# Scatter of the routed rows: 4 groups by 32 slot pairs, two 64-token products side by side, 4 KB row pieces

## The reference

```python
# layer 0, routed feed-forward: groups of 16 tokens, 64 slots a group
grouped = x.reshape(..., 16, d)
logits = einsum('...btd,des->...btes', grouped, controller) + tie
perm = (logits == max(logits, axis=-3, keepdims=True))      # which token fills a slot
sel = einsum('...btd,...btes->...besd', grouped, perm)
inner = relu(einsum('...besd,desf->...besf', sel, f1) + bias)
inter = einsum('...besf,esfd->...besd', inner, f2)
out = einsum('...besd,...btes->...btd', inter, perm)         # the scatter
x = x + tanh(g_ffn[0]) * out
# layer 1: softmax(layernorm(x) @ ctx.T / sqrt(512) + mask * -1e9) @ ctx, added to x;
# then a layer norm and an int8/ternary feed-forward whose scale is a quantile of |h|
```

## Time and profile before

| | value |
|---|---|
| median of three runs | 1633.4 us (1632.84 to 1636.59) |
| the profiled execution: its span | 1630.0 us, core 0, mean granted TensorE clock 0.894 |
| `phase2b3`, first to last instruction | about 845.4 to 1158.4 us |
| busy share of the span | PE 81%, DVE 63%, ACT 47%, POOL 27% |
| scatter products, L1197 | 256 records (two for each of 128 f32 products), 131.5 us |
| row loads, L1131 | 128 DMAs of 256 KB, median 5.5 us from issue to landing |

### The profile page before, as it was taken

One profiled execution on the slowest core, in us unless ns is written; L12 is line 12 of the kernel. 1 busy time (PEld: TensorE's weight loads), 2 busy tenths in 40 slices (PEclk: granted clock), 3 DMA queues, 4 the chain that ended last, 5 costly groups with the idle time before them and its releaser, 6 DMA issues. The chain is left out here.

```text
span 1630.0 us, 24926 instructions
## 1 busy us (share of the span) xinstructions
PE 1327.1 (81%) x8930; PEld 934.2 (57%) x8930; DVE 1032.4 (63%) x2374; ACT 759.7 (47%) x1145; POOL 432.6 (27%) x435
## 2 busy tenths in 40 slices
PE   6999999999999738999957999996141799343996
PEld 5787888878888527666524666664041444142442
DVE  5577666766667533444334778786496399776774
ACT  3233333333333212665333555554383655386991
POOL 1233333333323310110012787866100000000011
PEclk9999999999999968999978999998555699755998
DMA  6111222111221158787589988860300177421973
GB/s 217 46 66 67 73 84 103 65 71 66 94 93 40 40 213 293 261 300 271 219 305 278 256 238 231 235 183 29 121 1 3 78 310 305 162 78 51 419 311 149
DMA packets 100406, 261.79 MB, mean 161 GB/s; under 512 B 11120, under 2 KB 22480, under 8 KB 93136
## 3 DMA queue, kind: packets, MB, share of 16 engines
q1 hardware_dynamic: 88704, 226.82, 40.1%
q0 software_dynamic: 8688, 32.51, 5.8%
q10 hardware_dynamic: 2912, 1.14, 0.3%
HBM read 155.32 MB, written 105.12 MB: 160 GB/s over the span
## 5 line engine op out<-in xcount | busy, mean ns | idle before, releaser
L1197 PE MATMUL p_s<-p_rows,p_permT 128*128 128x512 f32 x256 | 131.5, 611 | 5.9 <-DMA p_rows<-inter_d 3.9
L916 PEld LDWEIGHTS p_sel<-p_pick,p_xp 128*128 128x128 bf16 x1536 | 89.5, 100 | 55.5 <-issue 34.2
L916 PE MATMUL p_sel<-p_pick,p_xp 128*128 128x128 bf16 x1536 | 100.9, 224 | 21.9 <-DMA p_xp<-xparts 19.3
L2261 POOL DMA_DIRECT2D p_y<-residual x8 | 10.0, 1254 | 405.4 <-POOLq L113 342.9
L1928 PE MATMUL p_z<-qT,w1T 128*128 128x512 bf16 x512 | 113.3, 385 | 2.1 <-PEq L113 2.1
L1054 DVE COPY p_selT<-p_sel 128x512 f32<-128x512 f32 x64 | 44.2, 691 | 104.5 <-PE p_sel L916 104.5
L2285 PE MATMUL p_o<-w2T,p_Gq 128*128 128x512 bf16 x384 | 85.9, 384 | 8.0 <-DVE p_Gq L2342 8.0
L1987 DVE MAX8 cand<-hid 128x8 f32<-128x128 f32 x384 | 74.7, 276 | 25.1 <-ACT hid L1975 25.1
L1928 PEld LDWEIGHTS p_z<-qT,w1T 128*128 128x128 bf16 x512 | 50.6, 99 | 64.7 <-issue 5.7
L999 ACT ACTIVATE p_selT<-p_sel 128x512 f32<-128x512 f32 x64 | 38.2, 597 | 88.3 <-PE p_sel L916 88.3
L341 PE MATMUL p_M<-p_ctxTh,p_Wkh 128*128 128x256 f32 x256 | 76.0, 297 | 1.9 <-DVE p_Wkl L663 1.9
(11 more groups left out here) (335 smaller groups left out, 3935.3 us busy)
## 6 DMA issues: line engine op xcount, KB each, us to landing
inter_d<-p_stage SPq DMA_DIRECT2D x64, 512.0 KB, 4.1
p_rows<-inter_d SPq DMA_DIRECT2D x128, 256.0 KB, 5.5
activations<-hid SPq DMA_DIRECT2D x24, 1024.0 KB, 3.9
p_cin<-in_ctx_dram SPq DMA_DIRECT2D x32, 512.0 KB, 5.1
xparts<-p_parts SPq DMA_DIRECT2D x16, 768.0 KB, 3.2
hid<-activations SPq DMA_DIRECT2D x10, 1024.0 KB, 9.1
p_xp<-xparts SPq DMA_DIRECT2D x3, 3072.0 KB, 24.9
p_xin<-in_x_dram SPq DMA_DIRECT2D x16, 512.0 KB, 4.2
```

The costliest lines, as they stand in the source:

```text
L916: mm = pe.matmul(bsel[u % 2][:, k * P:(k + 1) * P], xp[:, c, tile, r, :], pick[sb % 2][:, tile, :, :].rearrange("p s g -> p (s g)"), start ...
L1197: mm = pe.matmul(bo[t][:, :], permT[b % 2][:, t, k, :], R[b % 2][:, t, k, :], start=(k == 0), stop=(k == NK - 1))
```

## The change

Each tile's 512 rows are cut another way. The tile is halved, h = 0 and 1, by its groups (4 groups, 64 tokens each), and the slots go in pairs q = 0, 1. A block of 128 rows is 4 groups x 32 slot pairs, the same q of each pair, so a product of a block writes only the 64 tokens of its own half. Two such products, of h = 0 and h = 1, write partitions 0 to 63 and 64 to 127 of one bank, one issued right behind the other; two q accumulate. That is again 8 products per batch, each of 64 weight columns. `spread` and `permT` have half as many values (256 per token and tile), with a mask of 4 columns that DVE sums from the old one once; `turn_perm` has 4 transposes for 8. A tile's rows come by one DMA of 1 MB in 256 pieces of 4 KB, contiguous in DRAM, 2 DMAs per batch for 8.

```diff
-SK = 16
-NK = SL // SK
+GH = 4
+TH = P // 2
+ND = 2
...
-        rows = inter_d.rearrange("(n g) (k s) d -> n k s g d", g=GR, s=SK)
+        rows = inter_d.rearrange("(n h g) (s q) d -> n (g s) h (q d)", h=2, g=GH, q=ND)
...
             def load_rows(b, t):
-                for k in range(NK):
-                    sp.dma_start(R[b % 2][:, t, k, :], rows[b * NT + t, k]).then_inc(s[f"r_in{b % 2}{t}"], 16)
+                sp.dma_start(R[b % 2][:, t, :, :, :].rearrange("p h q d -> p h (q d)"), rows[b * NT + t]).then_inc(s[f"r_in{b % 2}{t}"], 16)
...
-                mm = pe.matmul(bo[t][:, :], permT[b % 2][:, t, k, :], R[b % 2][:, t, k, :], start=(k == 0), stop=(k == NK - 1))
-                if k == NK - 1:
+                for h in range(2):
+                    toks = slice(h * TH, (h + 1) * TH)
+                    mm = pe.matmul(bo[t][toks, :], permT[b % 2][:, t, q, toks], R[b % 2][:, t, h, q, :], start=(q == 0), stop=(q == ND - 1))
+                if q == ND - 1:
...
-                for k in range(NT * NK):
+                for k in range(NT * ND):
                     if i < B:
-                        scatter(i, k // NK, k % NK)
+                        scatter(i, k // ND, k % ND)
                     if k == 0 and live(i - 2):
                         scores(i - 2, 1)
-                    if k == 1 and i + 1 < B:
+                    if k == 0 and i + 1 < B:
                         turn_perm(i + 1)
-                    if k == 3 and live(i - 2):
+                    if k == 2 and live(i - 2):
                         turn_e(i - 2)
-                    if k == 4 and live(i - 1):
+                    if k == 2 and live(i - 1):
                         turn_xn(i - 1)
-                    if k == 5 and live(i - 2):
-                        attend(i - 2, 0)
-                    if k == 6 and live(i - 2):
-                        attend(i - 2, 1)
-                    if k == 6 and i < B:
-                        turn_ctx(i)
-                    if k == 7 and live(i - 1):
-                        scores(i - 1, 0)
+                if live(i - 2):
+                    attend(i - 2, 0)
+                    attend(i - 2, 1)
+                if i < B:
+                    turn_ctx(i)
+                if live(i - 1):
+                    scores(i - 1, 0)
...
+            pool.wait_ge(s["mask4_done"], 1)
...
+            dve.tensor_tensor(mask4[:, :], gmask[:, 0:GH], gmask[:, GH:GR], ALU.add).then_inc(s["mask4_done"], 1)
```

More of the change, by code:

```diff
@@ L1085, in phase2b3 @@
         sbt = lambda n, s, d=F32: es.enter_context(nc.sbuf_tensor("p3_" + n, s, d))
-        R = [sbt(f"rows{i}", [P, NT, NK, D]) for i in range(2)]
+        R = [sbt(f"rows{i}", [P, NT, 2, ND, D]) for i in range(2)]
         xy = [sbt(f"xy{i}", [P, NT, D]) for i in range(XD)]
-        spread = [sbt(f"spread{i}", [P, NT, SL, GR], BF16) for i in range(2)]
-        permT = [sbt(f"permT{i}", [P, NT, NK, P]) for i in range(2)]
+        spread = [sbt(f"spread{i}", [P, NT, ND, GH, SL // ND], BF16) for i in range(2)]
+        permT = [sbt(f"permT{i}", [P, NT, ND, P]) for i in range(2)]
+        mask4 = sbt("mask4", [P, GH])
         ident, identb = sbt("ident", [P, P]), sbt("identb", [P, P], BF16)
@@ L1188, in _, with scatter @@
         def _(pe):
-            def scatter(b, t, k):
-                if t == 0 and k == 0:
+            def scatter(b, t, q):
+                if t == 0 and q == 0:
                     pe.wait_ge(s["permT_done"], b + 1)
-                if k == 0:
-                    pe.wait_ge(s[f"r_in{b % 2}{t}"], 16 * NK * (b // 2 + 1))
+                if q == 0:
+                    pe.wait_ge(s[f"r_in{b % 2}{t}"], 16 * (b // 2 + 1))
                     if b >= 1:
                         pe.wait_ge(s["added"], NT * (b - 1) + t + 1)
-                mm = pe.matmul(bo[t][:, :], permT[b % 2][:, t, k, :], R[b % 2][:, t, k, :], start=(k == 0), stop=(k == NK - 1))
-                if k == NK - 1:
+                for h in range(2):
+                    toks = slice(h * TH, (h + 1) * TH)
+                    mm = pe.matmul(bo[t][toks, :], permT[b % 2][:, t, q, toks], R[b % 2][:, t, h, q, :], start=(q == 0), stop=(q == ND - 1))
+                if q == ND - 1:
                     mm.then_inc(s["scattered"], 1)
@@ L1205, in turn_perm @@
                 for t in range(NT):
-                    for k in range(NK):
-                        mm = pe.transpose(bP[:, :].bitcast(BF16)[:, (t * NK + k) * P:(t * NK + k + 1) * P],
-                                          spread[b % 2][:, t, k * SK:(k + 1) * SK, :].rearrange("p s g -> p (s g)"), identb[:, :])
+                    for q in range(ND):
+                        mm = pe.transpose(bP[:, :].bitcast(BF16)[:, (t * ND + q) * P:(t * ND + q + 1) * P],
+                                          spread[b % 2][:, t, q, :, :].rearrange("p g s -> p (g s)"), identb[:, :])
                 mm.then_inc(s["turned"], 1)
@@ L1289, in permT_out @@
                     act.wait_ge(s["scattered"], NT * (b - 1))
-                act.activation(permT[b % 2][:, :, :, :], bP[:, :].bitcast(BF16).rearrange("p (t k q) -> p t k q", t=NT, k=NK), ACT.Copy).then_inc(s["permT_done"], 1)
+                act.activation(permT[b % 2][:, :, :, :], bP[:, :].bitcast(BF16)[:, 0:NT * ND * P].rearrange("p (t q k) -> p t q k", t=NT, q=ND), ACT.Copy).then_inc(s["permT_done"], 1)
             def shifted(dst, src, rstd, minus, done, t):
@@ L1383, in spreads @@
                 for t in range(NT):
[L1384 to L1386 removed]
+                    v = pool.tensor_tensor(spread[b % 2][:, t, :, :, :],
+                                           perm[:, b * NT + t, :].rearrange("p (s a q) -> p q a s", a=1, q=ND).broadcast_to([P, ND, GH, SL // ND]),
+                                           mask4[:, :].rearrange("p (a g c) -> p a g c", a=1, c=1).broadcast_to([P, ND, GH, SL // ND]), ALU.mult)
                 v.then_inc(s["spread_done"], 1)
```

2 lines of the change are left out of this document (1 added, 1 removed).

## The result

The changed kernel took **1643.85 us** (median of 4 runs, 1642.49 to 1646.02) beside 1634.88 us of the kernel before on the same chip (4 runs, 1632.84 to 1636.59): ratio 1.0053, 95% interval 1.0038 to 1.0067. That is 9.0 us slower: half a percent, and clear of the noise. The profiled execution spans 1643.3 us for 1630.0, at a mean granted clock of 0.877 for 0.894.

A forecast was written before the change was run, and what follows sets the result against it. The step was taken as bound by a circle through DVE, POOL and ACT, without scatter. Span 1630.0 - 10.5 (start) + 1 (two early steps) + 20 (12 steady steps) = 1640.5, plus 3.4 for the median: 1644 us, range 1619 to 1653.

The forecast's parts named there:

- Rivals 3: Whole kernel: PE is the bound, so the end comes 55 us sooner, 1578 us; chance 0.03.
- 4 (no overlap): Scatter on PE: the pairs do not overlap, no idle time, step near 16.3 us, 1626 us; chance 0.06.
- rival 5: Row loads at the start: the rows are no faster, the rest as forecast, 1651 us; chance 0.09.
- The clock falls each step: Steady steps: PE idle 3.5 to 4.8 us ahead of turn_e restarts at or soon falls to half clock.
- rival 2: Steady steps: the clock holds, start and early steps gain, 1619 us; chance 0.17.
- L1501 loses its place: Steady steps: half clock at turn_e lets POOL's operation shut out DVE's scaling; 18.5 us, 2.2 more, in 7 steps.
- the second kind: Steady steps: half clock begins after turn_e, L1501 keeps its place, attend is late; 17.3 us in 5 steps.
- Rival 1: Steady steps: the clock falls but L1501 keeps its place, about 17.2 us each, 1634 us; chance 0.18.
- The start: Up to turn_e of step 2: loads 6.8, spreads 1.0 and scatter 2.7 us sooner, together -10.5 us.
- 17.3 us become 10.5: 6.8 us sooner: Start: 4.2 MB of rows queued ahead of POOL's gain vectors load at 400 GB/s for 243, 6.8 us sooner.
- Steps 2 and 3: The two steps before the steady ones: 14.8 us each at full clock, 16 to 17.5 at half; +1 us taken.
- the main term: The 12 steady steps 4 to 15: 216 us for 195.95, +20 us.

The follow-up runs named there:

- Experiment 3: The kernel before with four of its eight scatter products per batch left out, old shape and loads kept: 1643.52 us, ratio 1.0054.
- Experiments 5: The changed kernel with 24 idle products ahead of each turn_e, gain vectors loaded behind x, and the scaling on ACT: 1617.67 us, ratio 0.9895.
- 6: The changed kernel with 12 idle products ahead of each turn_e, gain vectors loaded behind x, and the scaling on ACT: 1617.59 us, ratio 0.9904.
- Experiment 1: The changed kernel with 24 idle products on PE just ahead of each turn_e: 1623.65 us, ratio 0.9934.
- experiment 7: Reordered ACT and POOL: 14 idle products 1641.68 us, kernel before 1641.63, changed kernel 1662.52; then another ACT order, 14 or 24 idle products: 1631.82, 1627.56.
- experiment 2: The changed kernel without DVE's scaling by tanh(g_xattn), the reciprocal written directly: 1635.58 us, ratio 1.0007.
- experiment 4: The changed kernel with the gain vectors loaded behind x and POOL waiting for them only at its first gains: 1641.29 us, ratio 1.0053.

## Why the prediction was right, and where it was not

**What bounds the kernel: right.** The prediction took the step for a circle through DVE, POOL and ACT that holds no scatter. Experiment 3 removed half of the scatter alone and gained nothing, though there the clock fell as well. Experiments 5 and 6 show it at full clock: idle time on PE that differs by 1.3 us leaves the step at 15.82 us, and 0.45 us taken off DVE's list shortens it by 0.28. Rivals 3 (PE the bound) and 4 (no overlap) fell with the first rows, and rival 5 (rows no faster) with the load rate.

**The clock falls each step: right, and shown as cause.** The foreseen wait was 3.5 to 4.8 us; it is 3.25 to 4.71 in steps 5 to 15, in seven of these eleven under 3.5. The clock over 960 to 1100 us is 0.88, above the foreseen 0.75 to 0.85: half clock lasts for a part of each step only. Experiment 1 took the wait away with useless work and got the clock and 22.7 us in twelve steps back; rival 2 described that kernel, but not the changed one. By the rule of the Trainium skill (TensorE: Matmul & The Clock Gate, HAM oscillation) on waits in a loop, every step pays; the trace of the changed kernel agrees: the clock of every steady step is 0.90 or less, and none is under 17.39 us for 16.33. With shorter waits in each step, of 0.91 to 2.26 us in the two kernels with 14 idle products in experiment 7, only some of the steps pay.

**L1501 loses its place: right in kind, one step out in number.** Forecast were 7 steps of 18.5 and 5 of 17.3, 216 us; measured 6 of 18.5 and 6 of 17.4, 215.58. Of the 19.6 us more, 13.0 are left without the scaling (208.96 us in experiment 2), which is the clock's share as near as it can be told, and 6.6 go with the collision. The price of the second kind, "nearly one us", was met by other parts than forecast: DVE takes `attended` 0 at T+5.79 for T+4.68, but `attend` ran at full clock, and the 1.1 us come from P3 and from `turn_xn`, whose 0.87 us more the sum left out. Rival 1 had the collision absent; experiment 2 made that case, at 1635.6 us for rival 1's 1634. The Trainium skill (SBUF — State Buffer, SBUF: two separate sides) speaks of a port pair that DVE and GpSimd hold in turn, each for a whole instruction, so that the other is fully blocked. The durations agree. The rule names DVE operations with two SBUF inputs or a fast mode; here it was a TENSOR_SCALAR on 128x2 f32 values, and no view shows in which mode it ran. Not every small operation is shut out: the reciprocal at 1008.24 took its usual 0.16 us inside POOL's operation of 1006.31 to 1008.67, while the scaling behind it ended at 1008.70, just past that one. The scalar per partition is not what makes the difference, since the negated maximum in experiment 7 has none and was shut out too; what does no run here shows.

**The start: mis-sized.** The step that failed is "17.3 us become 10.5: 6.8 us sooner". Counted from the phase's first record, the vectors reach POOL after 22.2 us for 26.1, 3.9 sooner. The rate was right: from 857 us on the rows come at some 400 GB/s. But the sum took the rate for the whole stretch. Windows of the changed kernel (the last three columns are clock, DMA share and GB/s):

```profile
847.00:849.00 2.00, 0.00 (x0) 0.00 (x0) 0.25 (x5) 0.00 (x0) 1.51 (x3) 0.50 0.32 51
853.00:855.00 2.00, 2.00 (x6) 0.39 (x7) 0.00 (x0) 0.00 (x0) 0.00 (x0) 0.50 0.30 84
857.00:859.00 2.00, 1.11 (x6) 0.48 (x8) 0.00 (x0) 0.00 (x0) 0.00 (x0) 1.00 1.04 404
```

Between 853 and 855 us the DMA engines are 0.30 busy. The place to compare is the one equally far behind the phase's first record: 5 to 7 us behind it the two microseconds carry 13 and 0 GB/s, and 197 and 91 in the kernel before, which has a shallower hole there. The deep hole is in experiments 1, 2 and 4 too. A second dip, to 145 and 291 GB/s, comes 19 to 21 us behind the first record, just before the vectors are there; experiment 4, with the vectors later in the queue, has 385 and 377 GB/s at that place. Counted at 400 GB/s (250 before), the first hole costs 1.1 us more than before and the dip 0.9: an estimate of 2.0 of the 2.9 us that are missing. The cause of neither was isolated, and stays open. The scatter of the start was forecast to give 2.7 us and the spreads 1.0; from the vectors to `turn_e` of step 2 it is 2.35 us less, not 3.7. With the loads' 3.9 that makes the 6.3 us. Experiment 4 shows what was left out: the rows of batch 2 are 1.7 us behind.

**Steps 2 and 3: wrong sign.** Forecast +1, measured -1.1. Step 2 ran at clock 1.00 and took 14.72 us, the 14.8 named for full clock. PE had waited 0.77 us ahead of its `turn_e`, and it waited 2.16 us ahead of that of step 3, which ran at 0.90 and took 16.37 us. The clock fell one step later than assumed.

**The sum.** The misses on the start (+4.2 against the forecast), on steps 2 and 3 (-2.1), on the twelve (-0.4), and +1.8 and -0.8 outside the change make 2.7 us: the span is 1643.3 for 1640.5. The median lies 0.5 us above the span, not 3.4 as before; the 3.4 were no fixed term but came from a fast profiled execution. So 1644 us was met in part because two errors of some 3 us cancel, which is luck. The sign and the size of the main term were not. Against the medians the change costs 9.0 us, for 10.5 forecast.

## What to carry to other kernels

An engine that looks busiest need not be the bound: a stretch in which it has less to do and the period stays the same, as in the earlier trace rows, tells it before any work is spent. Halving the work of an engine that waits already lengthens its wait, and on TensorE that can cost more than the work did; look at what a longer wait did to the clock elsewhere in the same trace, and if a wait can't be avoided, idle products in it can hold the clock. Twelve were enough in one order of the work and fourteen were not in two others, so the granted clock has to be read again after each change. Tiny operations of VectorE beside long ones of GpSimd belong where GpSimd waits, or on ScalarE, and a new order must be looked at for the next tiny one that lands inside.

## What the runs showed of the hardware

- TensorE's clock: waits of 1.84 to 1.87 us ahead of `turn_e` in each step left it at full (2.4 GHz) in experiment 6. Waits of 3.25 us and more in each step, in the changed kernel and in experiments 2 and 3, brought a clock of 0.78 to 0.90 over a step, with transposes of `turn_e` at up to 1.12 us for 0.66, as at 1.2 GHz. Between them it went both ways: after 2.17 us the next step ran at 1.00 in experiment 2, after 2.16 us at 0.90 in the changed kernel, and after 2.40 us at 0.89 and then at 1.00 in experiment 3. Two shorter waits in a step, 0.91 and 0.68 us, put it down in every other step of the last order of experiment 7.
- A TENSOR_SCALAR of DVE on 128x2 values takes 0.17 to 0.45 us, or up to 2.4 us when it starts within some hundredths of a microsecond of, or inside, a 128x1024 operation of POOL; it then ends with that operation. A shift of 0.3 us in its start made the difference. A RECIPROCAL of the same size took its 0.16 us inside such an operation.
- f32 products of 64 weight columns issued in pairs pass at 1.94 us for eight records of 512 columns; four of 128 took the same 1.94 us in the kernel before.
- Rows of 4 KB contiguous in DRAM load at 404 GB/s with the DMA engines full, pieces of 2 KB whose neighbours are 128 KB apart at 243, and the x and context loads at 400.
